# A decoder on one core: the mixers' decay mask as a matmul, the head scale on ScalarE, the norm weight folded into a projection, and the feed-forward's routing steps at other blocks

## The reference, cut to what matters

```python
# Mamba2 mixer: 4 heads of 128, state 128 (cut; chunked scan of the original)
zxbcdt = hidden @ in_proj_w.T                     # z, xBC, dt
xBC = silu(conv4(xBC)); dt = softplus(dt + dt_bias); A = -exp(A_log)
# per head: decay(t, s) = exp(sum of dt*A over s+1..t) for s <= t, else 0
# y[t] = sum_s (C[t] . B[s]) * decay(t, s) * dt[s] * x[s] + D * x[t]
g = y * silu(z)
rstd = rsqrt(mean(g * g over a head) + 1e-5)
out = ((g * rstd) * norm_w) @ out_proj_w.T
# cross attention: 16 heads over the 256 context positions' features, softmax, times gamma
# feed-forward: experts share W1, W2; two of eight are chosen per token
w, idx = top_k(softmax(x @ Wr + br), 2)
a_e = gelu(x @ W1 + b1 + (x @ A1_e) @ B1_e * 2)
out = sum_e w_e * (a_e @ W2 + b2 + (a_e @ A2_e) @ B2_e * 2)
```

## Time and profile before

| | |
|---|---|
| median of 3 runs | 3698.75 us (3693.86 to 3701.84) |
| profiled execution | 3698.53 us, span 3696.8 us |
| TensorE busy | 3280.0 us, 89% of the span; mean granted clock 0.928 |
| VectorE, ScalarE, GpSimd busy | 2312.1, 1551.7, 807.1 us |
| phases | mixers from about 2120 us, feed-forward from about 2990 us |

### The profile page before, as it was taken

One profiled execution on the slowest core, in us unless ns is written; L12 is line 12 of the kernel. 1 busy time (PEld: TensorE's weight loads), 2 busy tenths in 40 slices (PEclk: granted clock), 3 DMA queues, 4 the chain that ended last, 5 costly groups with the idle time before them and its releaser, 6 DMA issues. The chain is left out here.

```text
span 3696.8 us, 59668 instructions
## 1 busy us (share of the span) xinstructions
PE 3280.0 (89%) x21729; PEld 2552.8 (69%) x21729; DVE 2312.1 (63%) x4793; ACT 1551.7 (42%) x3486; POOL 807.1 (22%) x1031
## 2 busy tenths in 40 slices
PE   7898898989889779999999957979798879999999
PEld 5656566565656469889889835656566568888888
DVE  3544455454545567777777754858575667666666
ACT  2231322213222145555555423637464555555555
POOL 1221202212121211111111133332422112222222
PEclk9899999989989889999999977989899889999999
DMA  4000000000000066666676630301110022222222
GB/s 174 12 17 12 11 12 17 17 12 11 12 17 7 12 230 236 228 243 232 232 242 228 211 113 28 114 14 64 52 52 18 7 89 92 75 66 66 67 66 69
DMA packets 128035, 321.51 MB, mean 87 GB/s; under 512 B 37312, under 2 KB 37952, under 8 KB 118416
## 3 DMA queue, kind: packets, MB, share of 16 engines
q1 hardware_dynamic: 94192, 243.93, 19.6%
q0 software_dynamic: 19360, 50.46, 4.3%
q10 hardware_dynamic: 14336, 25.17, 1.9%
HBM read 277.32 MB, written 42.18 MB: 86 GB/s over the span
## 5 line engine op out<-in xcount | busy, mean ns | idle before, releaser
L1012 POOL DMA_INDIRECT xg<-normed_rows,idx x128 | 120.8, 944 | 675.1 <-PE psum L1094 633.2
L2171 POOL TENSOR_TENSOR mixf<-act 128x256 f32<-128x256 f32 x128 | 143.5, 1121 | 528.8 <-DVE act L2432 528.8
L1109 PE MATMUL psum<-xT_hi,wgu_hi 128*128 128x192 f32 (+1 forms) x1536 | 222.8, 267 | 2.0 <-DVE xT_lo L1154 2.0
L169 POOL TENSOR_SCALAR ve<-mv 128x1 f32<-128x1 f32 x112 | 37.8, 338 | 854.6 <-DVE mv L149 582.6
L1109 PE MATMUL psum<-xT_lo,wgu_hi 128*128 128x192 f32 (+1 forms) x1536 | 224.0, 268 | 0.0
L1109 PE MATMUL psum<-xT_hi,wgu_lo 128*128 128x192 f32 (+1 forms) x1536 | 223.3, 267 | 0.0
L1148 DVE TENSOR_TENSOR wgu_lo<-wgu,wgu_hi 128x1408 fp32r<-128x1408 f32 x128 | 202.4, 1622 | 21.8 <-ACT wgu_hi L1036 21.8
L1109 PEld LDWEIGHTS psum<-xT_hi,wgu_hi 128*128 128x128 f32 (+1 forms) x1536 | 196.3, 183 | 11.5 <-DVE xT_lo L1154 2.4
L1540 ACT ACTIVATE scratch<-psum,smin 128x512 f32<-128x512 f32 x256 | 173.8, 686 | 67.6 <-DVE smin L1934 65.4
L2432 DVE TENSOR_TENSOR act<-act,maskT 128x512 f32<-128x512 f32 x128 | 88.3, 689 | 171.2 <-ACT act L2209 171.0
L1109 PEld LDWEIGHTS psum<-xT_lo,wgu_hi 128*128 128x128 f32 (+1 forms) x1536 | 191.0, 183 | 0.0
(11 more groups left out here) (381 smaller groups left out, 8710.0 us busy)
## 6 DMA issues: line engine op xcount, KB each, us to landing
wgu<-in_w_gu_dram SPq DMA_DIRECT2D x64, 1408.0 KB, 6.1
wd<-in_w_d_dram SPq DMA_DIRECT2D x64, 512.0 KB, 8.3
w_raw<-in_w_dram SPq DMA_DIRECT2D x128, 256.0 KB, 2.6
expert_out<-yo ACTq DMA_DIRECT2D x64, 256.0 KB, 4.1
wd<-in_w_d_dram SPq DMA_DIRECT2D x64, 192.0 KB, 8.6
expert_out<-yo ACTq DMA_DIRECT2D x64, 128.0 KB, 4.4
up_raw<-in_w_up_dram SPq DMA_DIRECT2D x16, 384.0 KB, 3.4
xn<-in_x_dram SPq DMA_DIRECT2D x8, 512.0 KB, 3.6
```

The source lines that it names most:

```text
L1012: pool.indirect_dma_start(out=xg[b][0:w, t, :], out_offset=None, in_=rows, in_offset=bass.IndirectOffsetOnAxis(ap=idx[b][0:w, t:t + 1], ax ...
L1109: ins = pe.matmul(bank(2 + m)[0:w, gu * CAP:(gu + 1) * CAP], wgu2[b][wp][:, gu, kc, m0:m0 + w], xT2[b][xp][:, kc, :], start=(i == 0 and kc ...
L2171: pool.tensor_tensor(mixf[:, g % LAG, :], act2[:, g % LAG, 0, :], act2[:, g % LAG, 1, :], ALU.add).then_inc(sy["f_mix"], 1)
```

## The change

The mask becomes a matmul: a 128x384 tile `dropped_b` in bf16, 0 where a decay is kept and -1e30 where it is dropped, is multiplied by a bf16 identity into the PSUM bank first, and the three triangle products add to it, so the exponential gives 0 there; GpSimd's `masked_decay` is gone. `norm_bc` is gone: `w_mo` is multiplied once by the norm weight. The head's scale becomes two ScalarE copies with a scale, placed ahead of the squares; `context_high(first)` stands before the gates and `context_high(second)` at the loop's end. GpSimd makes both sequences' triangles before `context_low(first)`. The second projection's second product stands behind `scores(1)`. In the feed-forward, store and reload of `xo` go to blocks 3 and 4, `biased` to 6, `router` and `logits` to 7, `router_exp` to 8 (before the first gelu), `choose` to 8 and 9, mask turns and copies to 10 and 11, `masked` to 12, `m_lo` to 13. Weights, data and results are otherwise the same.

```diff
+        ident_b, dropped_b = sb("ident3_b", [P, P], BF16), sb("dropped_b", [P, 3 * P], BF16)
...
 
-            def masked_decay(k):
-                pool.wait_ge(sy["decay_ready"], k + 1)
-                pool.tensor_tensor(decay[:, k % 2, :], decay[:, k % 2, :], tri_le[:], ALU.mult
-                                   ).then_inc(sy["decaymask_ready"], 1)
-
             def gate_norm(k):
                 b, hd = (k // MH) % 2, k % MH
...
                 if more and p:
                     gather(first + 2)
                 triangles(first)
+                triangles(second)
                 context_low(first)
-                triangles(second)
-                k0 = 2 * MH * p
-                for k in range(2 * MH + 2):
-                    if k < 2 * MH:
-                        masked_decay(k0 + k)
-                    if k >= 2:
-                        gate_norm(k0 + k - 2)
+                for k in range(2 * MH):
+                    gate_norm(2 * MH * p + k)
                 for s in (first, second):
                     norm(s, norm2(s))
                 context_low(second)
...
                                          accum_out=ssq[b][:, j * MH + hd:j * MH + hd + 1])
                 ins.then_inc(sy["sumsq_ready"], 1)
 
+            def scaled(k):
+                b, hd = (k // MH) % 2, k % MH
+                act.wait_ge(sy["gated_norm"], k + 1)
+                for j in range(NT):
+                    head = y[b][:, j, hd * P:(hd + 1) * P]
+                    ins = act.activation(head, head, ACT.Copy, scale=grstd[b][:, j * MH + hd:j * MH + hd + 1])
+                    if hd == MH - 1:
+                        ins.then_inc(sy["attn_ready"], 1)
+
             def high(s, j):
                 act.wait_ge(sy["normed_ready"], NT * norm2(s) + j + 1)
                 act.activation(h2[s % 2][0][:, j, :], h[s % 2][:, j, :], ACT.Copy, scale=-LD_SCALE
...
                 else:
                     time_steps(*dt_calls(p)[0], dt_count(first))
                     convolved((first, second))
+                context_high(first)
                 gates(first)
                 gates(second)
-                context_high(first)
                 input_rows(first)
                 input_rows(second)
                 scaled_rows(first)
                 k0 = 2 * MH * p
-                for k in range(2 * MH + 2):
+                for k in range(2 * MH + 3):
                     if k < 2 * MH:
                         decays(k0 + k)
                     if k == 1:
                         scaled_rows(second)
-                    if k == 3:
+                    if k >= 3:
+                        scaled(k0 + k - 3)
+                    if 2 <= k < 2 * MH + 2:
+                        squares(k0 + k - 2)
+                    if k == 2 * MH + 1:
                         context_high(second)
-                    if k >= 2:
-                        squares(k0 + k - 2)
                 gated_copy(first)
                 gated_copy(second)
                 for j in range(NT):
...
-                pe.matmul(dec[:, 0:2 * P], tri[:, hd, 0, :], tri_le[:, 0:2 * P], start=True, stop=False,
+                pe.matmul(dec[:, 0:3 * P], ident_b[:], dropped_b[:], start=True, stop=True)
+                pe.matmul(dec[:, 0:2 * P], tri[:, hd, 0, :], tri_le[:, 0:2 * P], start=False, stop=True,
                           skip_group_check=True)
                 pe.matmul(dec[:, P:2 * P], tri[:, hd, 2, :], tri_le[:, 0:P], start=False, stop=True,
                           skip_group_check=True)
-                pe.matmul(dec[:, 2 * P:3 * P], tri[:, hd, 1, :], tri_le[:, 0:P], start=True, stop=True,
+                pe.matmul(dec[:, 2 * P:3 * P], tri[:, hd, 1, :], tri_le[:, 0:P], start=False, stop=True,
                           skip_group_check=True).then_inc(sy["decay_psum"], 1)
                 pe.matmul(prod[:, 0:2 * P], xbc[b][:, 1, 0:P], xbc[b][:, 2 + hd, :], start=True, stop=True)
                 pe.matmul(prod[:, 2 * P:3 * P], xbc[b][:, 1, P:S], xbc[b][:, 2 + hd, P:S], start=True, stop=True
...
                 b = s % 2
                 pe.wait_ge(sy["colsT_ready"], 8 * (s // 2) + 4 + NT * (b + 1))
-                for j in range(NT):
-                    project_pe(pe, bank(2 + 4 * b + j), lambda kc: hT[b][:, kc, j * P:(j + 1) * P],
-                               lambda kc: w_mo[:, kc, :]).then_inc(sy["out_psum"], 1)
+                project_pe(pe, bank(2 + 4 * b + j), lambda kc: hT[b][:, kc, j * P:(j + 1) * P],
+                           lambda kc: w_mo[:, kc, :]).then_inc(sy["out_psum"], 1)
 
             def scores(q):
                 b, n = (q // PAIRS) % 2, q % PAIRS
...
                 turn_gated(first)
-                project_out(first)
+                for j in range(NT):
+                    project_out(first, j)
                 turn_gated(second)
-                project_out(second)
+                project_out(second, 0)
                 q0 = HP * p
                 for i in range(HP + 3):
                     if i < HP:
                         scores(q0 + i)
+                    if i == 1:
+                        project_out(second, 1)
                     if 2 <= i < HP + 2:
                         turn_probs(q0 + i - 2)
                     if i >= 4 and i % 2 == 0:
...
                                              ).then_inc(sy["zs_ready"], 1)
 
             def weights(k):
-                dve.wait_ge(sy["decaymask_ready"], k + 1)
+                dve.wait_ge(sy["decay_ready"], k + 1)
                 dve.wait_ge(sy["bc_psum"], k + 1)
                 if k >= 2:
...
-                b, hd = (k // MH) % 2, k % MH
-                c = slice(hd * P, (hd + 1) * P)
-                dve.wait_ge(sy["gated_norm"], k + 1)
-                for j in range(NT):
-                    ins = dve.scalar_tensor_tensor(out=y[b][:, j, c], in0=y[b][:, j, c],
-                                                   scalar=grstd[b][:, j * MH + hd:j * MH + hd + 1],
-                                                   in1=norm_bc[:, c], op0=ALU.mult, op1=ALU.mult)
-                    if hd == MH - 1:
-                        ins.then_inc(sy["attn_ready"], 1)
 
             def residual(s, j):
...
             ln(dve.tensor_scalar(small[:, 0:30], small[:, 0:30], 0.5, None, ALU.mult))
+            ln(dve.tensor_copy(ident_b[:], ident))
+            ln(dve.tensor_scalar(dropped_b[:], tri_le[:], -1.0, -NEG, ALU.add, ALU.mult))
+            for kc in range(KC):
+                ln(dve.tensor_scalar(w_mo[:, kc, :], w_mo[:, kc, :], norm_w[:, kc:kc + 1], None, ALU.mult))
             for p in range(npair):
...
                     gates(s)
                 k0 = 2 * MH * p
-                for k in range(2 * MH + 3):
+                for k in range(2 * MH + 2):
                     if k < 2 * MH:
                         weights(k0 + k)
-                    if 2 <= k < 2 * MH + 2:
+                    if k >= 2:
                         gated(k0 + k - 2)
-                    if k >= 3:
-                        scaled(k0 + k - 3)
                 for j in range(NT):
                     residual(first, j)
                 for j in range(NT):
...
                         sp.wait_ge(sy["f_hT_psum"], NT * (s + 1))
                         load_x(s + 1)
-                    if f == 6:
+                    if f == 3:
                         if s:
                             sp.wait_ge(sy["f_out_ready"], NT * s)
                             sp.dma_start(dr["out"][s - 1].rearrange("(t p) d -> p t d", p=P), xo[:]
                                          ).then_inc(sy["f_out_done"], 16)
-                    if f == 8:
+                    if f == 4:
                         if s:
                             sp.wait_ge(sy["f_out_done"], 16 * s)
                         sp.dma_start(xo[:], dr["mixed"][s]).then_inc(sy["f_xo_in"], 16)
...
                 if f == LAG - 1 and s >= 1:
                     t2m_hi(s - 1)
+                if f == 8 and s + 1 < nseq:
+                    router_exp(s + 1)
...
                         turned_hi(s + 1, f - 5)
-                    if f == 9:
-                        router_exp(s + 1)
-                    if f in (11, 12):
-                        mask_copy(s + 1, f - 11)
+                    if f in (10, 11):
+                        mask_copy(s + 1, f - 10)
                     if f == 13:
                         m_hi(s + 1)
 
...
-                    if f == 8:
+                    if f == 7:
                         router(s + 1)
-                    if f in (11, 12):
-                        turn_masks(s + 1, f - 11)
+                    if f in (10, 11):
+                        turn_masks(s + 1, f - 10)
                 if T2_LAG <= g < last + T2_LAG:
                     lora_down(g - T2_LAG)
                 if LAG <= g < last + LAG:
...
                     out(s - 1)
-                if f == 9 and s < nseq:
+                if f == 6 and s < nseq:
                     biased(s)
                 if s + 1 < nseq:
...
```

(32 more changed lines are left out.)

4 lines of the change are left out of this document (2 added, 2 removed).

## The result

| | before | after |
|---|---|---|
| median | 3696.31 us (3687.34 to 3701.84, 4 runs) | 3571.23 us (3566.85 to 3584.36, 4 runs) |
| profiled execution; span | 3698.5; 3696.8 us | 3566.9; 3565.1 us |
| mean granted clock | 0.928 | 0.947 |

The ratio is 0.9672, 95% interval 0.9643 to 0.9701: 125 us faster by the medians, 121 by the ratio. (A fourth run of the kernel before moved its median from 3698.75 to 3696.31.) The forecast was 3591, so 107 faster, with 3576 as the low end. The direction was right and most of the working holds; one term of the sum was far too small.

A forecast was written before the change was run, and what follows sets the result against it. It took the mixers' head loop to be bound by a circle through GpSimd's mask and the feed-forward by TensorE: 3698.5 - 71 (four pairs of 17.8) - 36 (feed-forward) = 3591 us, range 3576 to 3635.

The forecast's parts named there:

- Step 1: Mixers' head loop: with the mask off GpSimd the period falls from 4.37 to 2.78 us; the mask's matmul booked at nothing.
- Step 2: Head loop's start and run: first product 8.2 us earlier, seven steps 17.2 instead of 27.4 us; last product 18.4 earlier.
- Step 3: Head loop's end: ScalarE's queue delays the turned gate's copy to 8.8 us after the last product, a 2.9 us loss.
- Step 5: Norm weight folded into the projection weights, once, on VectorE: worth nothing; without cover 3 us.
- Step 6: Feed-forward: the wait for mrow in block 11 goes, a 1.5 us router wait comes; 36 us gained in sum.
- step 4: Second projection: one product behind the second scores fills 2.86 us of idle time, delays the third scores 0.7; gain 2.8.
- low end: The range's lower bound, 3576: 3591 less 15, for no new router wait (10) and a better level in the projections (5).
- The 0.5 us a pair booked for starting at 1.2 GHz: Loss booked because TensorE's idle stretch before the first projection grows from 3 to some 7 us.
- Unhidden mask matmul: Head loop: the mask's product adds 0.2 to 0.7 us a head, 6 to 21 us in all; 3605, chance 0.12.
- The feed-forward's hole only moves: Feed-forward: the router's wait or late choosing gives back up to the whole 36 us; 3627, chance 0.13.
- Half-level TensorE in the head loop: TensorE stays at 1.2 GHz in the head loop and bounds it; gain only 44 us, 3655, chance 0.08.
- Slower through the level over the dense part: Attention and feed-forward: more work at 1.2 GHz eats the 107 us won; 3741 with 300 us more, chance 0.03.

The follow-up runs named there:

- experiment 8: The changed kernel with the mask's matmul issued three times instead of once; 3573.39 us, ratio 0.9669.
- experiment 4: The kernel before with the feed-forward's part of the change alone; 3665.32 us, ratio 0.9910.
- experiment 5: The changed kernel with the residual's bias at block 6 moved behind the low part of the turned rows; 3551.03 us, ratio 0.9615.
- experiment 2: The kernel before with only the move of the second projection's second product behind scores(1); 3665.93 us against 3701.10, ratio 0.9913.
- Experiment 3: The kernel before with one projection product repeated behind scores(1) into a free bank, its result unread; 3676.18 us, ratio 0.9940.
- experiment 1: The changed kernel with both products of the second projection put back ahead of scores(0); 3615.67 us, ratio 0.9774.

## Why the prediction was right and where it failed

**Right, with its numbers.** Step 1 (period 2.78, measured 2.73; the mask's matmul free in the period, experiment 8). Step 2 (8.2 us earlier at the start and 10.2 in the loop; measured 33 and 40 us over four pairs). Step 3 (copy 8.8 us after the last product: exactly that). Step 5: nothing of it shows.

**Right in part by luck.** Step 2's working does not give its 17.2 us: 3.3 + 2.8 + 2.8 + 4 x 2.78 is 20.0. The figure holds because the first of the seven steps is only 0.47 us, the second 2.9 and the others 2.73, which is 17.1. Step 6 has the right sum (36; 34 by the profiles, 36 alone in experiment 4) from two errors that nearly cancel. Its wait at the router was booked at 1.5 us a sequence and measured 1.3, but taking it away won 20 us and not 9 (experiment 5). So the rest of step 6 is worth some 54 us where the sum had 47. By the windows of the kernel before and of experiment 5 TensorE is idle for 34 us less and busy for 19 us less; the 1.7 us of lower level booked for each sequence make 12 of these 19.

**The step that failed is step 4**, the projection: "It fills 2.86 of idle time; the rest, 0.7, delays the third scores. Gain 2.8." That is the hole alone; the term for the level behind it was put at nothing. In the third pair of the kernel before, TensorE worked at 1.2 GHz without a gap from 2698.51 to about 2710.8, and the other pairs have such a stretch too; the changed kernel does the same work in 5.5 us less. Measured by itself the move is worth 8 to 9 us a pair instead of 2.8 (experiment 2: 32 to 35 us, where the sum had 11). Experiment 3, which fills the hole and moves nothing, wins the 5.5 us (less the 0.7 that the filling costs), so they come from the idle time ahead of them and not from the tighter head loop. With 5.5 us more in each pair the prediction's sum would have been 3569, against the measured 3571. The 0.5 us a pair booked for starting at 1.2 GHz had the right mechanism at the wrong stall and a tenth of the size. The sign stood in the earlier trace rows: the third scores' row reads 0.79 us for two matmuls; a look at the same line a few us on, at 0.50, would have given the term.

The same error sits in the range. The low end took 10 us for the absence of the router's wait; experiment 5 measured 20, nine of idle time and nine of level in its trace. A low end that priced each wait at twice its length would have been 3566, with the result inside, but only by luck, since the router's wait did come and the missing gain was made elsewhere.

**The rivals.** Unhidden mask matmul: excluded by experiment 8. The feed-forward's hole only moves: of the 31.5 us of waiting for `mrow` in the seven sequences 8.9 came back at the router, over a quarter, and they cost 20. Half-level TensorE in the head loop: no, its products take the 2.4 GHz time, save for a short stretch in the second pair, whose loop took 18.6 us instead of 17.1. Slower through the level over the dense part: the opposite happened, the mean clock rose from 0.928 to 0.947. The prediction weighed the level mainly as a danger; what it missed was the level as a gain.

## What to carry to other kernels

Price an idle stretch of TensorE as itself plus the time lost at the lower clock behind it, a little under half of how long that clock lasts; the durations of one matmul line just behind the stretch and later show how long that is. Here 2.9 us of idle time cost about 8.3 (2.8 and 5.5), and 1.3 us ahead of the router cost 2.9 (20 us in seven sequences). Where the engine is the bound, look for the level as a gain of removing a hole, and not only as a danger. A piece of real work moved into the hole is the cheap remedy. Filling with work that nobody needs won 20 to 25 us in one place, 5 to 8 (by the traces) in another and nothing measurable in a third, so measure it.

## What was not expected of the hardware

After the 2.86 us hole TensorE ran at 1.2 GHz for 12.3 us though it had no gap in them. In experiment 1 the attention's time at the lower level was 14 us in two pairs, 20 in the fourth and 31 in the first (mean clock 0.84 over 95.8 us), behind the same hole. And the same stretch of the same code can run at the full level in one execution and partly at the lower one in another: the first pair's attention took 85.0, 86.0, 86.1 or 87.5 us, and the changed kernel's feed-forward 645.2 to 648.8 us in six traces. A gain of a few us that comes from the level is therefore not to be read from one trace.
